# RWKV feed-forward: two explicitly mixed rows from GpSimd in place of doubled products, and a moved receptance product

## The chip, the cores and the metric

The kernel runs on one core of one Trainium2 chip, as one launch. The metric is the device time of that launch in microseconds (us). Differences of less than about 0.3% can't be told from no change. In the text TensorE is PE, VectorE is DVE, ScalarE is ACT, GpSimd is POOL; "L1948" is line 1948 of the kernel before.

## The reference, cut to what matters

The program is a chain of four networks (cross attention with an MLP, an instance-norm attention, a second cross attention with an MLP, an RWKV block) over x of 16 sequences x 64 tokens x 256 channels. The change lies in the last one, the RWKV block, and there in its feed-forward half:

```python
def step(s, rkvw):
    r_t, k_t, v_t, w_t = rkvw
    a = k_t[..., :, None] * v_t[..., None, :]
    out = jnp.einsum('bhi,bhij->bhj', r_t, u * a + s)
    s = a + w_t[..., :, None] * s
    return (s, out)
...
og = ((og - m) / jnp.sqrt(va + 1e-05)).reshape(b, l, e) * gn_w + gn_b
x1 = x + og * g @ Wo.T
xc = _ln(x1, ln2_w, ln2_b)
sx2 = jnp.concatenate([state[:, 0:1] - xc[:, :1], xc[:, :-1] - xc[:, 1:]], axis=1)
xk2 = xc + sx2 * ffn_maa_k
xr2 = xc + sx2 * ffn_maa_r
rr = jax.nn.sigmoid(xr2 @ Wfr.T)
kk = jnp.square(jax.nn.relu(xk2 @ Wfk.T))
return x1 + rr * (kk @ Wfv.T)
```

`sx2` is the row before minus the row itself; `xk2` and `xr2` are the two mixed rows.

## The kernel before, in words

Everything but the inputs and outputs stays in SBUF. The 1024 rows are cut into 8 tiles of 128 rows (two sequences of 64), numbered 0 to 7 (`LAST` = 7). The five engines run their own programs, written out by hand in one order each, and are tied by semaphores: a step increments its signal (`did(i)`), and whoever needs it waits (`at(i)`). Each engine works strictly in its written order, so a wait holds all that stands behind it.

The RWKV part is a software pipeline over slots. In one slot PE works at several tiles at once; in the loop of `rwkv_tensor` (from L2130) it runs gather(slot-3), turn(slot), decay2 and spread1(slot-2), center(slot-3), ffn_keys and ffn_receive(slot-5), project(slot-1), turn_heads(slot-3), ffn2(slot-5), lora(slot), turn_ffn(slot-4), attended(slot-3), decay1(slot-1), mixes(slot), spread0(slot-1). The last tiles leave the loop and are finished by a straight list (L2160 to L2187), in which ffn_keys(5) stands ahead of gather(7), and whose `warm` calls (L270) are products whose result nobody reads.

The names the text needs:
- DVE, `rwkv_vector`: products0/products1 (L2457), bonus (L2498), out_heads (L2503), mix2 (L2441), group_sum (L2510), scan0/scan1 (L2476, 3 and 5 scans), group_rstd and group_norm (L2516, L2523), receive (L2492, the receptance times the scans of its 5 heads), gate (L2450), attended (L2529, makes x1), ffn and close (L2537, L2543), mix1 (L2433).
- ACT, `rwkv_scalar`: heads (L2265, gives `y`), f_stats (L2307 to L2311), f_normed (L230), square and std (L2253, L2258), ffn_rows (L2275, writes `xc`), relu, receive and relu_square (L2282, L2289, L2294).
- POOL, `rwkv_gpsimd`: f_rstd (L2616 to L2620), first (L2650), receive (L2657, the receptance times the scans of the other 3 heads, `rs0`), f_state (L2643), gated (L2664, which lets PE's attended start), bonus (L2671, `ruk`).

The feed-forward before the change needs no mixed row. Since xc + (xs - xc) f = xc (1-f) + xs f with xs the row before, POOL scales the weights once, early in the program (`rwkv_consts_gpsimd`, L1935 to L1940), and PE multiplies the same buffer `xc` (64 rows and the one before them, for two sequences) twice, read at offset 1 with W(1-f) and at offset 0 with Wf:

```python
ffn_parts = [(m.wr[:, W_FK, :, :], m.wr[:, W_FR, :, :], k, 1) for k in range(KD)]\
    + [(m.wfks, m.wfrs, k, 0) for k in range(KD)]
```

So ffn_keys is 8 products of 128x128 and ffn_receive is 8 products of 64 stationary columns by 256. In a trace each f32 product leaves two records.

turn_ffn(i) writes a PSUM bank that the tile before uses, and waits until DVE's ffn(i-1) has read it (`rf`, L2087).

## Time and profile before

| what | value |
|---|---|
| time, median of 3 runs (all) | 982.9 us (982.54, 982.9, 985.4) |
| span of the profiled execution | 982.8 us |
| PE busy / PE weight load busy | 944.6 (96%) / 795.7 (81%) |
| DVE / ACT / POOL busy | 592.1 (60%) / 462.5 (47%) / 411.8 (42%) |
| chain that ended last | PE 74%, DVE 12%, ACT 5%, issue 4%, POOL 4% |
| RWKV part | from about 807 us to the end |

Of the profiled execution the page gives the span alone; its 982.8 us is 0.1 us from the median run. The page cuts the span into busy shares, follows back the chain of work that ended last, and lists groups of instructions with what ended the idle time before them. Matmuls are pipelined and their ends are modelled, so the weight load is read beside PE's busy time.

### The profile page before, as it was taken

The page shows a single profiled execution, that of the slowest core. Times are in us where ns is not written, and L with a number is a line of the kernel's source. Part 1 is how long each engine was busy: PE and PEld are TensorE (multiplying, and loading weights), DVE is VectorE, ACT ScalarE, POOL GpSimd, SP SyncE. Part 2 cuts the span into 40 slices and gives each one's busy share as a digit, 9 for nine tenths or more (in the row PEclk, how much of TensorE's full clock was granted, in tenths as well). Part 3 has the DMA queues.
Part 4 walks back from the last instruction along what each step waited for, and adds up shares of the span by engine and source line. Part 5 has one row for each costly group of instructions (what it writes and reads, how often), then busy time and mean ns, then how long its engine had stood idle before and what let it go on. Part 6 is the DMA issues. An engine that isn't in the chain of part 4 may idle for free.

```text
span 982.8 us, 21494 instructions
## 1 busy us (share of the span) xinstructions
PE 944.6 (96%) x8321; PEld 795.7 (81%) x8321; DVE 592.1 (60%) x974; ACT 462.5 (47%) x1026; POOL 411.8 (42%) x572
## 2 busy tenths in 40 slices
PE   6999999989999999999999999999999999999998
PEld 4777777966788888988897888998888888678776
DVE  5899986767544433344356433344426766999883
ACT  4677874237643333333334333333342434576565
POOL 2143346875365333333246343342422862344231
PEclk9999999999999999999999999999999999999999
DMA  9100000310011110111101110111100100000000
GB/s 298 37 23 2 2 2 22 116 54 2 1 55 50 54 50 25 37 54 48 54 7 55 50 54 21 42 49 48 54 22 18 41 14 1 1 2 6 13 6 23
DMA packets 24147, 37.15 MB, mean 38 GB/s; under 512 B 4432, under 2 KB 16528, under 8 KB 23824
## 3 DMA queue, kind: packets, MB, share of 16 engines
q1 hardware_dynamic: 24080, 36.23, 11.9%
q8 instruction: 45, 0.74, 0.3%
q14 instruction: 22, 0.18, 0.1%
HBM read 35.17 MB, written 1.05 MB: 37 GB/s over the span
## 4 chain that ended last, share of the span: by engine, by line
PE 74%; DVE 12%; ACT 5%; issue 4%; POOL 4%; DMA 0%; DVEq 0%; ACTq 0%; POOLq 0%
PE ps L1292 18%; PE ps L790 13%; PE ps L1309 9%; PE ps L1351 6%; PE ps L1948 5%; PE ps L890 4%; PE ps L1327 4%; PE ps L1337 2%; DVE sb L2476 2%; DVE sb L656 1%; PE ps L270 1%; DVE sb L650 1%; PE ps L2026 1%; PE ps L421 1%; PE ps L2112 1%
## 5 line engine op out<-in xcount | busy, mean ns | idle before, releaser
L837 POOL TENSOR_TENSOR sb<-sb 128x256 fp32r<-128x256 f32 (+1 forms) x128 | 102.5, 801 | 278.0 <-DMA sb<-in_heads_a 144.9
L1292 PE MATMUL ps<-sb 128*128 128x512 f32 x768 | 187.7, 396 | 1.0 <-issue 1.0
L1292 PEld LDWEIGHTS ps<-sb 128*128 128x128 f32 x768 | 139.5, 188 | 33.0 <-ACT sb L1425 3.1
L790 PE MATMUL ps<-sb 128*128 128x256 f32 x1152 | 148.4, 286 | 0.0
L790 PEld LDWEIGHTS ps<-sb 128*128 128x128 f32 x1152 | 141.4, 191 | 2.1 <-issue 0.2
L839 POOL TENSOR_TENSOR sb<-sb 128x256 fp32r<-128x256 f32 (+1 forms) x128 | 115.8, 905 | 10.0
L1522 DVE SCALAR_TENSOR_TENSOR sb<-ps,sb 128x512 fp32r<-128x512 f32 x64 | 45.1, 747 | 95.6 <-ACT sb L1458 95.5
L1309 PE MATMUL ps<-sb 128*128 128x256 f32 x768 | 99.2, 285 | 0.4 <-DVE sb L1490 0.4
L1502 DVE TENSOR_REDUCE sb<-ps 128x8 f32<-128x520 f32 x32 | 22.4, 700 | 126.6 <-PE ps L1327 126.6
L1309 PEld LDWEIGHTS ps<-sb 128*128 128x128 f32 x768 | 95.0, 191 | 3.0 <-issue 0.9
L1425 ACT ACTIVATE sb<-ps,sb 128x512 f32<-128x512 f32 x64 | 43.8, 685 | 107.9 <-PE ps L1292 107.8
L1948 PE MATMUL ps<-sb 128*128 128x128 f32 (+2 forms) x576 | 79.5, 290 | 3.9 <-DVE sb L2457 1.8
L1948 PEld LDWEIGHTS ps<-sb 128*128 128x128 f32 (+1 forms) x576 | 69.7, 185 | 12.9 <-issue 6.7
L1458 ACT ACTIVATE sb<-ps,sb 128x512 fp32r<-128x512 f32 x64 | 40.5, 684 | 80.6 <-PE ps L1351 80.6
L1490 DVE TENSOR_TENSOR sb<-ps,sb 128x512 f32<-128x512 f32 x64 | 43.9, 690 | 37.6 <-PE ps L1309 37.3
L1351 PEld LDWEIGHTS ps<-sb 64*128 64x128 f32 x1024 | 59.7, 188 | 8.1 <-issue 5.1
L1351 PE MATMUL ps<-sb 64*128 64x64 f32 x1024 | 64.1, 275 | 0.0
L2476 DVE TENSOR_TENSOR_SCAN sb<-sb 128x256 f32<-128x256 f32 x64 | 51.3, 863 | 0.0
L1442 ACT ACTIVATE sb<-ps,sb 128x512 f32<-128x512 f32 x64 | 43.4, 679 | 14.9 <-PE ps L1292 14.8
L1447 ACT ACTIVATE sb<-sb 128x520 f32<-128x520 f32 x32 | 20.5, 640 | 63.1 <-DVE sb L1504 63.1
L890 PE MATMUL ps<-sb 128*128 128x512 f32 x192 | 47.9, 403 | 0.0
L222 POOL TENSOR_TENSOR sb<-sb 128x1 f32<-128x1 f32 x24 | 13.3, 554 | 81.7 <-DVE sb L606 74.0
(221 smaller groups left out, 1668.2 us busy)
## 6 DMA issues: line engine op xcount, KB each, us to landing
sb<-in_heads_a SPq DMA_DIRECT2D x32, 386.0 KB, 3.0
sb<-in_heads_c SPq DMA_DIRECT2D x16, 256.0 KB, 3.6
...
```

The source lines that it names most:

```text
L790: last = pe.matmul(m.acc(t), lhsT[x], rhs[w], start=opens and n == 0, stop=False, skip_group_check=True)
L837: pool.tensor_tensor(high, src, one, ALU.mult).then_inc(*G.did(name + "_high", u))
L839: pool.tensor_tensor(low, src, high.bitcast(F32), ALU.subtract).then_inc(*G.did(name, u))
L890: last = pe.matmul(m.ps[u][:, at, :], m.w_parts[u][w][:, (r % 2 * KD + k) * P:(r % 2 * KD + k + 1) * P], m.h_parts[x][:, k, c * 512:(c + 1 ...
L1292: last = pe.matmul(m.ps[u][:, c, :], m.w_parts[u][w][:, (KD * q + k) * P:(KD * q + k + 1) * P], rows[x][:, k, c * 512:(c + 1) * 512], star ...
L1309: last = pe.matmul(m.ps[u0][:, c0, b * 2 * P:(b + 1) * 2 * P], m.enc_parts[x][:, k, (2 * j + b) * P:(2 * j + b + 1) * P], m.wv_parts[w][:, ...
L1351: last = pe.matmul(m.ps[1 - u][:, o, j * P + b * S:j * P + (b + 1) * S], m.v[j // 2][half, 2 * (j % 2) + b, u, :], m.pT[u][half, j, b * S: ...
L1425: act.activation(head_keys_of(m, u)[:, 8 * c:8 * c + 8, 0:S], m.ps[u][:, c, :].rearrange("p (n k) -> p n k", k=S), ACT.Identity, bias=m.he ...
L1490: vec.tensor_tensor(dst, m.ps[u0][:, c0, :].rearrange("p (b c) -> p b c", b=2), bc(m.v_row[:, :], 1, [P, 2, 2 * P]), ALU.add).then_inc(*hd ...
L1522: vec.scalar_tensor_tensor(out=m.ctx_low(u, o), in0=m.ctx_ps(u, o), scalar=m.bv[u][:, :], in1=m.ctx_high(u, o).bitcast(F32), op0=ALU.add, ...
L1948: last = pe.matmul(out, lhsT, rhs, start=n == 0, stop=n == len(terms) - 1)
L2476: last = vec.tensor_tensor_scan(m.sc[:, j, :], m.wS[i % 2][:, :, :].rearrange("p n s -> p (n s)"), m.av[:, j, :, :].rearrange("p n s -> p ...
```

## The change

`xc` gets a companion: for each tile two full mixed rows are written into a new buffer `xkr` (two of them, by tile parity, in the place of the scaled weights), with `sx2` as scratch. For tiles 0 to 5 POOL makes them (one subtraction of 128x256, one product and one sum of 128x512), at the end of its slot; for tiles 6 and 7 (`BY_VECTOR`) DVE does (one subtraction of 128x256 and four fused multiply-adds of 128x128), at two places of its closing list. PE then has 4 products of 128x128 for the keys and 2 of 128 stationary columns by 256 for the receptance, both behind the new signal `xkr`. POOL's receptance product (`receive`) moves behind `gated` in each slot. The early scaling of the weights goes, but for `headsum_u`. `ffn_rows` and `f_state` of the next tile wait for `xkr` of the last instead of for its receptance product.

```diff
+BY_VECTOR = range(LAST - 1, TILES)
@@ rwkv_consts_gpsimd
-    pool.tensor_tensor(m.wfks, m.wr[:, W_FK, :, :], wide("ffn_k", D), ALU.mult)
-    pool.tensor_tensor(m.wfrs, m.wr[:, W_FR, :, :], wide("ffn_r", D), ALU.mult)
     pool.tensor_tensor(m.headsum_u, bc(m.headsum[:, :], 1, [P, KD, P]), wide("u", P), ALU.mult).then_inc(m.s_scaled, 1)
-    pool.wait_ge(m.s_scaled, 1)
-    pool.tensor_tensor(m.wr[:, W_FK, :, :], m.wr[:, W_FK, :, :], m.wfks, ALU.subtract)
-    pool.tensor_tensor(m.wr[:, W_FR, :, :], m.wr[:, W_FR, :, :], m.wfrs, ALU.subtract).then_inc(m.s_scaled, 1)
@@ rwkv_tensor
     def ffn_keys(i):
-        pe.wait_ge(*done["xc"].at(i))
-        pe.wait_ge(*done["f_state"].at(i))
+        pe.wait_ge(*done["xkr"].at(i))
         for e in range(KD):
             last = product(m.key_bank(i)[:, e * P:(e + 1) * P],
-                           [(wk[:, k, e * P:(e + 1) * P], m.xc[:, k, :, s:s + S]) for wk, _, k, s in ffn_parts])
+                           [(m.wr[:, W_FK, k, e * P:(e + 1) * P], m.xkr[i % 2][:, 0, k, :]) for k in range(KD)])
...
-        for n, (_, wr, k, s) in enumerate(ffn_parts):
-            for b in range(2):
-                last = pe.matmul(m.receive_bank(i)[b * S:(b + 1) * S, D:2 * D], m.xc[:, k, b, s:s + S], wr[:, k, :],
-                                 start=n == 0, stop=n == len(ffn_parts) - 1)
-        last.then_inc(*done["kk_rr"].did(i))
+        product(m.receive_bank(i)[:, D:2 * D],
+                [(m.xkr[i % 2][:, 1, k, :], m.wr[:, W_FR, k, :]) for k in range(KD)]).then_inc(*done["kk_rr"].did(i))
@@ rwkv_scalar, ffn_rows
-            act.wait_ge(*done["kk_rr"].at(i - 1))
+            act.wait_ge(*done["xkr"].at(i - 1))
@@ rwkv_vector
+    def ffn_mix(i):
+        vec.wait_ge(*done["xc"].at(i))
+        vec.wait_ge(*done["f_state"].at(i))
+        if i == BY_VECTOR[0]:
+            vec.wait_ge(*done["xkr"].at(i - 1))
+        vec.tensor_tensor(m.sx2..., rows[:, :, 0:S], rows[:, :, 1:S + 1], ALU.subtract)
+        vec.wait_ge(*done["kk_rr"].at(i - 2))
+        for f, name in enumerate(("ffn_k", "ffn_r")):
+            for k in range(KD):
+                last = vec.scalar_tensor_tensor(out=split(m.xkr[i % 2][:, f, k, :]), in0=split(m.sx2[:, k, :]),
+                                                scalar=m.col(name, k), in1=m.xc[:, k, :, 1:S + 1], op0=ALU.mult,
+                                                op1=ALU.add)
+        last.then_inc(*done["xkr"].did(i))
@@ the closing list
     group_norm(LAST)
+    ffn_mix(LAST - 1)
     attended(LAST)
-    for i in (LAST - 2, LAST - 1, LAST):
+    ffn(LAST - 2)
+    close(LAST - 2)
+    ffn_mix(LAST)
+    for i in (LAST - 1, LAST):
         ffn(i)
         close(i)
@@ rwkv_gpsimd
     def f_state(i):
-            pool.wait_ge(*done["kk_rr"].at(i - 1))
+            pool.wait_ge(*done["xkr"].at(i - 1))
+    def ffn_mix(i):
+        pool.wait_ge(*done["xc"].at(i))
+        pool.wait_ge(*done["f_state"].at(i))
+        pool.tensor_tensor(m.sx2..., rows[:, :, 0:S], rows[:, :, 1:S + 1], ALU.subtract)
+        if i >= 2:
+            pool.wait_ge(*done["kk_rr"].at(i - 2))
+        pool.tensor_tensor(m.xkr[i % 2], bc(m.sx2, 1, [P, 2, KD, P]), bc(factors, 3, [P, 2, KD, P]), ALU.mult)
+        pool.tensor_tensor(mixed, mixed, bc(rows[:, :, 1:S + 1], 1, [P, 2, 4, S]), ALU.add)\
+            .then_inc(*done["xkr"].did(i))
@@ the loop over slots
         first(slot - 4)
+        gated(slot - 5)
         receive(slot - 4)
         f_state(slot - 6)
-        gated(slot - 5)
         bonus(slot - 3)
+        ffn_mix_early(slot - 6)
```

On POOL, one slot of the closing part (the one with gated(6) and the first 3 heads' product of tile 7). Before; `rwkv_y` is ACT's heads, `rwkv_scan0` DVE's first three scans:

```order
L2616 TENSOR_SCALAR sb<-sb 128x1 [waits attn0_rows_eps]
L2618 TENSOR_TENSOR sb<-sb 128x1 [waits gpsimd_own]
L2620 TENSOR_TENSOR sb<-sb 128x1 [waits gpsimd_own]
L2650 COPY sb<-sb 128x32 [waits rwkv_scan1]
L2657 TENSOR_TENSOR sb<-sb 128x768 [waits rwkv_scan0]
L2643 COPY sb<-sb 128x4 [waits rwkv_kk_rr]
L2664 TENSOR_TENSOR sb<-sb 128x256 [waits rwkv_gate,rwkv_y]
```

The same slot with the change (`attn0_ctx` is the semaphore that carries `xkr`):

```order
L2629 TENSOR_SCALAR sb<-sb 128x1 [waits attn0_rows_eps]
L2631 TENSOR_TENSOR sb<-sb 128x1 [waits gpsimd_own]
L2633 TENSOR_TENSOR sb<-sb 128x1 [waits gpsimd_own]
L2687 COPY sb<-sb 128x32 [waits rwkv_scan1]
L2701 TENSOR_TENSOR sb<-sb 128x256 [waits rwkv_gate,rwkv_y]
L2694 TENSOR_TENSOR sb<-sb 128x768 [waits rwkv_scan0]
L2657 COPY sb<-sb 128x4 [waits attn0_ctx]
L2664 TENSOR_TENSOR sb<-sb 128x256 [waits rwkv_f_state,rwkv_xc]
L2670 TENSOR_TENSOR sb<-sb 128x512 [waits rwkv_kk_rr,gpsimd_own]
L2674 TENSOR_TENSOR sb<-sb 128x512 [waits gpsimd_own]
```

The product for 3 heads now follows gated, and the three instructions of the mix end the slot.

On PE, the closing list around gather(7), before: attended(6), ffn_keys(5), gather(7).

```order
L1948 MATMUL ps<-sb 128x256 [waits rwkv_gated]
L1948 MATMUL ps<-sb 128x256
L1948 MATMUL ps<-sb 128x128 [waits rwkv_f_state,rwkv_xc]
L1948 MATMUL ps<-sb 128x128 x7
L2050 MATMUL ps<-sb 128x128 [waits rwkv_x1,rwkv_ruk]
L2050 MATMUL ps<-sb 128x128
L2056 MATMUL ps<-sb 32x256 [waits rwkv_rs1,rwkv_rs0]
```

With the change:

```order
L1944 MATMUL ps<-sb 128x256 [waits rwkv_gated]
L1944 MATMUL ps<-sb 128x256
L1944 MATMUL ps<-sb 128x128 [waits attn0_ctx]
L1944 MATMUL ps<-sb 128x128 x3
L2046 MATMUL ps<-sb 128x128 [waits rwkv_x1,rwkv_ruk]
L2046 MATMUL ps<-sb 128x128
L2052 MATMUL ps<-sb 32x256 [waits rwkv_rs1,rwkv_rs0]
```

The order is the same; ffn_keys(5) has half the products and another wait.

## Rows read from the trace of the kernel before

**Rows 1.** The page, chain that ended last: share of the span by engine.
```profile
PE 74%; DVE 12%; ACT 5%; issue 4%; POOL 4%; DMA 0%; DVEq 0%; ACTq 0%; POOLq 0%
```

**Rows 2.** Windows: stretch, its length, PE, weight load, DVE, ACT, POOL busy (count); clock, DMA.
```profile
888.00:906.70 18.70, 18.70 (x160) 14.94 (x159) 16.84 (x26) 12.87 (x34) 6.89 (x13) 1.00 0.02 8
```

**Rows 3.** Chain that ended last, slot 6 (start us, us, what): keys, then receptance.
```profile
897.93 1.79 PE ps L1948 x16
899.72 1.88 PE ps L2112 x16
```

**Rows 4.** Timeline, slot 6: start us, us, engine, line [idle before <-releaser].
```profile
902.38 4.16 DVE L2476 TENSOR_TENSOR_SCAN sb<-sb 128x256 f32<-128x256 f32 x5
906.49 0.42 DVE L2537 SCALAR_TENSOR_TENSOR sb<-sb,ps 128x256 f32<-128x256 f32 x1
906.82 1.77 DVE L2492 TENSOR_TENSOR sb<-sb 128x1280 f32<-128x1280 f32 x1
907.48 1.70 POOL L2671 TENSOR_TENSOR sb<-sb 128x256 f32<-128x256 f32 x1 [0.23 <-ACT sb L2234]
907.85 0.44 PE L2089 MATMUL ps<-sb 128*128 128x128 f32 x2
909.19 0.42 DVE L2529 TENSOR_TENSOR sb<-ps,sb 128x256 f32<-128x256 f32 x1 [0.27 <-PE ps L1948]
911.30 1.49 DVE L2433 TENSOR_TENSOR sb<-ps,sb 128x1280 f32<-128x1280 f32 x1 [1.36 <-PE ps L1987]
```

**Rows 5.** Timeline, slot 4, the same POOL line; then all scans: duration ns min/median/max.
```profile
870.31 0.72 POOL L2671 TENSOR_TENSOR sb<-sb 128x256 f32<-128x256 f32 x1 [0.97 <-ACT sb L2234]
...
L2476 DVE TENSOR_TENSOR_SCAN sb<-sb x64: 657/665/2235, 831.7 to 958.6; 128x256 f32<-128x256 f32 x64
```

**Rows 6.** By source line, POOL's 128x512 product and difference: ns min/median/max, first and last start.
```profile
L1936 POOL TENSOR_TENSOR sb<-sb x1: 1490/1490/1490, 312.4 to 312.4; 128x512 f32<-128x512 f32 x1
...
L1939 POOL TENSOR_TENSOR sb<-sb x1: 1282/1282/1282, 314.6 to 314.6; 128x512 f32<-128x512 f32 x1
```

**Rows 7.** Timeline, closing part, tiles 4 to 7.
```profile
946.34 0.79 ACT L2275 ACTIVATE sb<-ps,sb 128x128 f32<-128x128 f32 x2
...
948.49 0.19 POOL L2616 TENSOR_SCALAR sb<-sb 128x1 f32<-128x1 f32 x1 [2.18 <-ACT sb L2311]
...
950.62 0.59 ACT L230 ACTIVATE sb<-sb 128x256 f32<-128x256 f32 x1
...
951.35 0.38 ACT L2253 ACTIVATE sb<-ps 128x256 f32<-128x256 f32 x1
...
951.84 0.41 DVE L2510 TENSOR_REDUCE sb<-sb 128x32 f32<-128x256 f32 x1
...
954.10 1.82 POOL L2657 TENSOR_TENSOR sb<-sb 128x768 f32<-128x768 f32 x1 [4.34 <-DVE sb L2476]
...
955.60 0.80 ACT L2265 ACTIVATE sb<-ps,sb 128x128 f32<-128x128 f32 x2
...
959.52 1.47 DVE L2492 TENSOR_TENSOR sb<-sb 128x1280 f32<-128x1280 f32 x1
...
961.14 1.07 PE L2056 MATMUL ps<-sb 128*32 128x256 f32 x16 [0.15 <-DVE sb L2492]
...
962.27 0.42 DVE L2498 TENSOR_TENSOR sb<-ps,sb 128x256 f32<-128x256 f32 x1 [0.49 <-PE ps L2056]
```

**Rows 8.** Timeline: DVE's two fused multiply-adds of 128x128; ACT's last ffn_rows; PE's last ffn2.
```profile
899.38 0.62 DVE L2421 SCALAR_TENSOR_TENSOR sb<-sb 128x128 f32<-128x128 f32 x2
...
973.78 0.81 ACT L2275 ACTIVATE sb<-ps,sb 128x128 f32<-128x128 f32 x2
...
978.67 1.13 PE L1948 MATMUL ps<-sb 128*128 128x256 f32 x4
```

**Rows 9.** Windows, PE alone: stretch, length, busy (count), granted clock, DMA share, GB/s.
```profile
762.90:764.60 1.70, 0.00 (x0) 1.00 0.00 0
766.00:769.70 3.70, 3.70 (x11) 0.54 0.00 0
```

More of the change, by code:

```diff
@@ L2090, in turn_ffn @@
         last.then_inc(*done["f_turned"].did(i))
-    ffn_parts = [(m.wr[:, W_FK, :, :], m.wr[:, W_FR, :, :], k, 1) for k in range(KD)]\
-        + [(m.wfks, m.wfrs, k, 0) for k in range(KD)]
     @of_tile
     def ffn_keys(i):
-        pe.wait_ge(*done["xc"].at(i))
-        pe.wait_ge(*done["f_state"].at(i))
+        pe.wait_ge(*done["xkr"].at(i))
         for e in range(KD):
             last = product(m.key_bank(i)[:, e * P:(e + 1) * P],
-                           [(wk[:, k, e * P:(e + 1) * P], m.xc[:, k, :, s:s + S]) for wk, _, k, s in ffn_parts])
+                           [(m.wr[:, W_FK, k, e * P:(e + 1) * P], m.xkr[i % 2][:, 0, k, :]) for k in range(KD)])
         last.then_inc(*done["kk_raw"].did(i))
@@ L2529, in attended @@
         vec.tensor_tensor(m.x[:, i, :], m.c0[:, 0:D], m.x[:, i, :], ALU.add).then_inc(*done["x1"].did(i))
+    def ffn_mix(i):
+        rows = m.xc[:, :, :, :].rearrange("p k b s -> p (k b) s")
+        split = lambda x: x.rearrange("p (b s) -> p b s", b=2)
+        vec.wait_ge(*done["xc"].at(i))
+        vec.wait_ge(*done["f_state"].at(i))
+        if i == BY_VECTOR[0]:
+            vec.wait_ge(*done["xkr"].at(i - 1))
+        vec.tensor_tensor(m.sx2.rearrange("p k (b s) -> p (k b) s", b=2), rows[:, :, 0:S], rows[:, :, 1:S + 1],
+                          ALU.subtract).then_inc(*m.own_vec.did("sx2", i))
+        vec.wait_ge(*m.own_vec.at("sx2", i))
+        vec.wait_ge(*done["kk_rr"].at(i - 2))
[5 more added lines that the diff above has]
+        last.then_inc(*done["xkr"].did(i))
     @of_tile
@@ L2641, in f_state, with ffn_mix_early @@
         if i >= 1:
-            pool.wait_ge(*done["kk_rr"].at(i - 1))
+            pool.wait_ge(*done["xkr"].at(i - 1))
         pool.tensor_copy(m.xc[:, :, :, 0], state(i, 0)).then_inc(*done["f_state"].did(i))
+    def ffn_mix(i):
+        rows = m.xc[:, :, :, :].rearrange("p k b s -> p (k b) s")
+        pool.wait_ge(*done["xc"].at(i))
+        pool.wait_ge(*done["f_state"].at(i))
+        pool.tensor_tensor(m.sx2.rearrange("p k (b s) -> p (k b) s", b=2), rows[:, :, 0:S], rows[:, :, 1:S + 1],
+                           ALU.subtract).then_inc(*m.own_pool.did("sx2", i))
+        pool.wait_ge(*m.own_pool.at("sx2", i))
+        if i >= 2:
+            pool.wait_ge(*done["kk_rr"].at(i - 2))
+        factors = m.colbuf[:, COL["ffn_k"]:COL["ffn_k"] + 2 * KD].rearrange("p (f k) -> p f k", f=2)
+        pool.tensor_tensor(m.xkr[i % 2], bc(m.sx2, 1, [P, 2, KD, P]), bc(factors, 3, [P, 2, KD, P]), ALU.mult)\
+            .then_inc(*m.own_pool.did("sxf", i))
+        pool.wait_ge(*m.own_pool.at("sxf", i))
+        mixed = m.xkr[i % 2].rearrange("p f k (b s) -> p f (k b) s", b=2)
+        pool.tensor_tensor(mixed, mixed, bc(rows[:, :, 1:S + 1], 1, [P, 2, 4, S]), ALU.add)\
+            .then_inc(*done["xkr"].did(i))
+    @of_tile
+    def ffn_mix_early(i):
+        if i not in BY_VECTOR:
+            ffn_mix(i)
     @of_tile
@@ L2807, in build @@
         scaled = lambda at, n: consts[:, at:at + KD * n].rearrange("p (k n) -> p k n", k=KD)
-        m.wfks, m.wfrs, m.headsum_u = (
-            scaled(at, n) for at, n in ((0, D), (KD * D, D), (KD * 2 * D, P)))
+        m.xkr = [consts[:, at:at + 2 * D].rearrange("p (f k n) -> p f k n", f=2, k=KD) for at in (0, KD * D)]
+        m.headsum_u = scaled(KD * 2 * D, P)
+        m.sx2 = scaled(KD * (2 * D + 3 * P), P)
         m.xl = [scaled(at, P) for at in (KD * (2 * D + P), KD * (2 * D + 2 * P))]
@@ L2876, in build @@
         m.tile_done["kk_raw"] = Signal(m.done["ctx_ps"].sem, len(ITEMS))
+        m.tile_done["xkr"] = Signal(m.done["ctx"].sem, len(ITEMS))
         m.own_vec, m.own_act, m.own_pool = (Own(sem(n)) for n in ("vector_own", "scalar_own", "gpsimd_own"))
@@ L3012, in _ @@
             mlp_tensor(pe, ph["mlp2"], m, 12, HALVES[:-LATE])
-            rwkv_tensor(pe, m, ph["mlp2"], 12, [(m.s_scaled, 2)])
+            rwkv_tensor(pe, m, ph["mlp2"], 12, [(m.s_scaled, 1)])
 def lay_out(inputs):
```

## The prediction

> **What bounds the kernel now.** I read the page first: the chain that ended last is PE's to 74%, DVE's to 12% [rows 1]. The change touches nothing before 807 us but five lines of POOL at 311 us, so I then cut the RWKV part into slots. In a middle slot of 18.7 us PE is busy all of it and DVE 16.84 us [rows 2]. In the chain the middle slots are PE alone, one row after another; the keys and the receptance stand in it with 1.79 and 1.88 us per tile [rows 3]. The timeline of the slot shows how close the others are: DVE waits only twice, 0.27 us for attended and 1.36 us for mixes [rows 4]. So the middle is PE's with DVE 1.6 us behind.
>
> The Trainium skill (Perfetto Trace Analysis, Identifying the Most-Contended Engine) holds PE's weight load, not its busy time, for the measure of how full it is. By that the slot is 14.94 of 18.7 us, 80% [rows 2], less full than it looks; the sum below goes by DVE's waits and needs neither.
>
> The closing part is a chain over all engines: DVE's scans and product (959.52), gather(7) on PE (961.14), bonus on DVE (962.27) [rows 7], then gate by gate to the last ffn2 at 978.67 [rows 8].
>
> **The change part by part.**
>
> *The products.* Keys go from 8 products to 4, receptance from 8 of half width to 2 of full width, that is half of 1.79+1.88 [rows 3]: about 1.85 us less of PE per tile.
>
> *What a middle slot gains.* Not 1.85: DVE's two waits are 1.63 us in all, and a second bound stands in front. turn_ffn(i) waits for DVE's ffn (L2537, at 906.49), which stands behind the five scans; it now runs at 907.85 [rows 4]. A slot can thus shrink by 907.85 - 906.49 - 0.42 = 0.94 us before PE waits there. POOL adds to that. Its product L2671 takes 0.72 us alone and 1.70 us beside DVE's two-input L2492, which itself takes 1.77 us against 1.47 elsewhere [rows 4, 5, 7]; one scan takes 0.665 us in the median and up to 2.235 [rows 5]. So instructions of POOL and of DVE with two SBUF inputs hold each other up. The moved receptance product (1.82 us, [rows 7]) now meets L2492 instead of the scans: DVE's scans gain perhaps 0.5 us and L2492 loses up to 1.8. And f_rstd now stands behind the mix, about 1 us late, so f_normed, and behind it on ACT square, and then group_sum on DVE, slip by some 0.3 to 0.6. I take 0.65 us per slot for the two full slots and 0.6 for the slot after them (there DVE waits 0.57 for PE): **-1.9 us**; ends -4 (all of DVE's waits go, with the scans' gain) and +0.5 (POOL's blocking eats it).
>
> The Trainium skill (SBUF, SBUF: two separate sides) says of the port pair that the two engines share that the loser "fully blocks" for a whole instruction. The pair 0.72 and 1.70 us agrees; by that rule, with one meeting of the 1.8 us product and L2492 per slot, the slots would gain nothing and the sum would be 1.9 us higher.
>
> *The mix on POOL.* No row shows it. The nearest are its own 128x256 product (0.72, [rows 5]) and the 128x512 product and difference of the constants (1.49 and 1.28, [rows 6]): 3.5 us a tile with the two own waits between; ends 3.2 and, where L2492 stands in the way, 5. In middle slots it starts when `xc` is there and ends some 2 us ahead of ffn_keys; hidden, with f_rstd queued behind it as counted.
>
> *Tile 4's mix, closing part.* `xc`(4) is there at 947.13, the mix ends at 950.7. f_rstd(5), begun at 948.49, now begins there: 1.1 us later it lets f_normed(5) start at 951.8 instead of 950.62; square(6) comes at 952.4 instead of 951.35 and group_sum(6) at 952.9 instead of 951.84 [rows 7]. DVE's scans for tile 7 stand behind it: the chain is **1.1 us** late, and ACT's heads(6) starts at 956.7 instead of 955.60.
>
> *Tile 5's mix.* This is the large one. POOL's order is now gated(6), receive(7), f_state(5), mix(5). gated(6) waits for heads(6) (957.5) and for a scan under way, and ends near 958.9; receive(7) takes 1.82 plus one scan's blocking, to 961.2; L2492, due at 960.6, holds POOL to 962.6; the mix ends at 966.2. On PE ffn_keys(5) stands ahead of gather(7): 0.95 us, then gather with 1.7 us, so that DVE's bonus starts at 968.9 instead of 962.27 [rows 7]: **+6.6 us**, the 1.1 above in it. Lower end: no late group_sum and no blocking, 956.4 + 0.75 + 1.82 + 0.2 + 3.3 + 2.65 = 965.1, +2.9. Upper end: L2492 of tile 6 is held by POOL's product too, another 1.4, +8.
>
> *PE's clock.* With keys(5) late PE stands idle some 6 us behind attended(6). The trace has such a case: PE is idle for 1.7 us up to 764.6, and from 766.0 on, though busy without a gap, it has a mean of 0.54 of its clock for 3.7 us, the lower of the levels 1.2 and 2.4 GHz [rows 9]. That costs 3.7 x 0.46 = 1.7; It would fall on keys(5), gather(7) and center(7), all on the chain: **+1.7**, ends 0 and +3.8 (a second gap).
>
> *Tiles 6 and 7 on DVE.* One subtraction (0.42) and four multiply-adds (0.62 for two, [rows 8]) are about 1.8 us. For tile 6 they stand ahead of attended(7), waiting for `xc`(6), which ACT makes after heads(7): x1(7) slips by **0.3**. For tile 7 `xc` is there at 974.59 [rows 8]; then mix 1.85, keys and receptance 1.9 in place of 0.3 of waiting and 3.77 of products: **-0.25**.
>
> *The constants.* POOL loses 4 instructions of about 1.3 us at 311 us [rows 6]; the next ones wait for DMA and for PE there, so nothing. If that cover were gone it would be a gain of at most 5 us of POOL time, none of it on the chain.
>
> Sum: -1.9 + 6.6 + 1.7 + 0.3 - 0.25 = +6.45. On the profiled execution's 982.8 that is 989.25; the median of the runs is 0.1 above it: **989.3 us**.
>
> **The rivals.**
> - *The middle pays for the end* (no measurable change, within 0.3%, which is about what can be told from no change): slots gain 4, the end loses its lower 2.9 and no clock, up to the case gain 2, loss 4.5. 982 to 985.8 us. For it: DVE's 1.36 us waits are plain in the rows, and my blocking is counted from few meetings. Against: ffn_keys(5) ahead of gather(7) is in the order itself, and the moved product is in front of the mix. 0.22.
> - *PE's time counts in full* (faster): the middle is PE's to the last tenth [rows 2]; if turn_ffn's bound moves with the scans, four slots give 1.6 us each, and the end gives back its 1.85 us for tiles 4 and 7 while POOL gets tile 5's rows done by 962. It decides for this case if xkr(5) is ready before about 961.5, when gather(7) is due: then 982.9 - 6.5 - 1 + 0.5 = 976 us, or 979 with half of it. Against: gated(6) can't start before heads(6) at 956.4, and 1.82 + 3.3 us come behind it. 0.08.
> - *POOL slows the middle too*: blocking of L2492 and late group_sum exceed 1.6 us per slot. Then 989.3 + 1.9 + 1 = 992.2 us. For it: the 2.235 us scan [rows 5]. 0.15.
> - *The clock holds*, 987.6 us: it lies in the forecast's case.
>
> **How the numbers follow.** Forecast 0.55 (986 to 991.5), rivals as above. Faster 0.08, same 0.22, slower 0.70. The range that leaves out 2 in 10 reaches from 984.0 into the balance case to 993.0.
>
> **What would show it.** In the changed profile: slots of 18.0 us where 18.75 stand; PE no longer full in them, with a wait for DVE's ffn ahead of turn_ffn; POOL's mix of 3.5 us ending 2 us ahead of ffn_keys; group_sum(6) about 1 us late; PE idle some 6 us for POOL's L2674 ahead of ffn_keys(5), the longest wait of the part, with the clock at 0.5 behind it; from bonus(7) to the end 18 to 20 us as before. It is wrong if ffn_keys(5) does not wait for POOL, or if the slots stay at 18.75, or shrink to 17.

## The result

The changed kernel takes 989.96 us, median of 5 runs (989.55 to 991.39), against 982.9 (982.54 to 985.4) before: ratio 1.0059, 95% interval 1.0040 to 1.0077. The forecast was 989.3, slower. So the number is right, and the sections below show that this is in part luck: two of its terms were off by 2.4 to 3.2 us in opposite directions. The profiled execution is the longest of the five (span 989.6; the other four 987.7 to 988.3); a likely reason is in its trace and is told at the end of this section.

The page of the changed kernel, in answer to [rows 1]: span, busy time, and the chain that ended last.

```profile
span 989.6 us, 21204 instructions
PE 936.9 (95%) x8161; PEld 790.2 (80%) x8161; DVE 592.1 (60%) x984; ACT 462.1 (47%) x1026; POOL 430.2 (43%) x586
PE 63%; POOL 12%; DVE 11%; issue 8%; ACT 6%; DMA 0%; POOLq 0%; DVEq 0%; ACTq 0%
```

80 products fewer (160 records), and POOL's share of the chain goes from 4% to 12%, PE's from 74% to 63%. To see where, I follow one marker, DVE's bonus of each tile (L2498 before, L2488 after), through the RWKV part. Its starts for tiles 0 to 7 are, before: 842.62, 859.35, 876.53, 895.28, 914.04, 932.79, 949.04, 962.27; after: 843.36, 860.13, 878.72, 895.94, 913.15, 930.37, 944.67, 966.54. The last instruction of DVE starts at 980.29 and 987.03. Three stretches follow:

| stretch | before | after | difference | forecast |
|---|---|---|---|---|
| start of the part (bonus of tile 0) | 842.62 | 843.36 | +0.74 | 0 |
| bonus(0) to bonus(6), the middle | 106.42 | 101.31 | -5.11 | -1.9 |
| bonus(6) to bonus(7), the closing part | 13.23 | 21.87 | +8.64 | +6.6 and +1.7 |
| bonus(7) to the last close | 18.02 | 20.49 | +2.47 | +0.3 - 0.25 |

*The middle.* A full slot (from the bonus of tile 2 to that of tile 5 there are three) goes from 18.75 to 17.2 us, not to 18.0; the one behind them, bonus(5) to bonus(6), from 16.25 to 14.30. Windows over one slot, in answer to [rows 2]:

```profile
893.20:910.40 17.20, 16.67 (x140) 13.71 (x140) 16.97 (x26) 12.89 (x34) 11.25 (x16) 1.00 0.03 9
```

PE is busy for 16.67 of 17.2 us, DVE for 16.97: the slot is now DVE's (before, 18.70 and 16.84 of 18.7). Timeline of it, in answer to [rows 4] (the lines' numbers are ten lower: L2466 the scans, L2546 ffn, L2482 the receive rows, L2519 attended, L2423 mixes; on PE L2085 turn_ffn; on POOL L2694 the receive product and L2674 the mix's last; `...` marks rows left out):

```profile
903.02 3.51 DVE L2466 TENSOR_TENSOR_SCAN sb<-sb 128x256 f32<-128x256 f32 x5
...
906.46 0.39 DVE L2546 SCALAR_TENSOR_TENSOR sb<-sb,ps 128x256 f32<-128x256 f32 x1
906.77 2.72 DVE L2482 TENSOR_TENSOR sb<-sb 128x1280 f32<-128x1280 f32 x1
...
909.74 0.41 DVE L2519 TENSOR_TENSOR sb<-ps,sb 128x256 f32<-128x256 f32 x1
...
910.43 1.48 DVE L2423 TENSOR_TENSOR sb<-ps,sb 128x1280 f32<-128x1280 f32 x1
...
905.94 2.20 POOL L2694 TENSOR_TENSOR sb<-sb 128x768 f32<-128x768 f32 x1
...
912.18 1.19 POOL L2674 TENSOR_TENSOR sb<-sb 128x512 f32<-128x512 f32 x1
...
906.99 0.41 PE L2085 MATMUL ps<-sb 128*128 128x128 f32 x2 [0.53 <-DVE sb L2546]
```

Both waits of DVE are gone (0.27 and 1.36), the five scans take 3.51 instead of 4.16, L2482 takes 2.72 instead of 1.77 beside the moved product, and PE waits 0.53 for ffn ahead of turn_ffn, as forecast.

*The closing part.* Timeline, in answer to [rows 7]:

```profile
948.21 0.60 ACT L230 ACTIVATE sb<-sb 128x256 f32<-128x256 f32 x1 [1.86 <-POOL sb L2633]
...
949.11 0.42 DVE L2500 TENSOR_REDUCE sb<-sb 128x32 f32<-128x256 f32 x1 [1.55 <-ACT sb L2242]
...
953.72 1.15 POOL L2701 TENSOR_TENSOR sb<-sb 128x256 f32<-128x256 f32 x1 [5.37 <-ACT sb L2254]
954.82 2.19 POOL L2694 TENSOR_TENSOR sb<-sb 128x768 f32<-128x768 f32 x1
956.97 1.52 POOL L2657 COPY sb<-sb 128x4 f32<-128x4 f32 x1
958.63 0.61 POOL L2664 TENSOR_TENSOR sb<-sb 128x256 f32<-128x256 f32 x1
959.32 1.10 POOL L2670 TENSOR_TENSOR sb<-sb 128x512 f32<-128x512 f32 x1
960.50 1.17 POOL L2674 TENSOR_TENSOR sb<-sb 128x512 f32<-128x512 f32 x1
...
961.73 2.07 PE L1944 MATMUL ps<-sb 128*128 128x128 f32 x8 [5.15 <-POOL sb L2674]
...
964.59 1.87 PE L2052 MATMUL ps<-sb 128*32 128x256 f32 x16
...
966.54 0.43 DVE L2488 TENSOR_TENSOR sb<-ps,sb 128x256 f32<-128x256 f32 x1 [7.02 <-PE ps L2052]
```

group_sum(6) waits 1.55 us for ACT, which waits for POOL's f_rstd (L2633) behind the mix of tile 4. Then PE waits 5.15 us for the mix of tile 5, gather(7) follows behind its keys at 963.60, and DVE stands 7.02 us. The mix itself (958.63 to 961.67) takes 3.0 us. Windows, PE alone (stretch, length, busy, granted clock, DMA share, GB/s):

```profile
954.00:958.00 4.00, 2.58 (x7) 0.75 0.00 0
960.00:966.00 6.00, 4.27 (x28) 0.50 0.06 22
980.00:986.00 6.00, 4.95 (x16) 0.50 0.06 22
```

The clock is at its lower level, 1.2 of 2.4 GHz, not once but three times (953 to 956, 960 to 966, 980 to 986); the last time it hits the keys, receptance and products of tile 7, behind which nothing is left to hide it. The forecast had one fall of 1.7 us, and a second only as an upper end.

*The profiled execution.* The slot from the bonus of tile 1 to that of tile 2 takes 18.59 us in this trace. Six other traces, below, of kernels with the same order there (in y2 with a mix of one column) have 17.38 or 17.39 (before: 17.18); in this one the clock is 0.50 at 864 to 866. I take the 1.2 us for an event of this execution, since the other four are 1.3 to 1.9 us shorter; that is argued, for they left no trace. The middle's gain without it is 6.3 us.

### The profile page after: what moved, and what is told of

It reads as the page before. It is cut to its first block, busy times and chain, and to the rows that moved or that the text cites. A ratio compares the mean times of both kernels' runs of the same rounds, so it can differ in the third digit from the quotient of the medians.

```text
span 989.6 us, 21204 instructions
## 1 busy us (share of the span) xinstructions
PE 936.9 (95%) x8161; PEld 790.2 (80%) x8161; DVE 592.1 (60%) x984; ACT 462.1 (47%) x1026; POOL 430.2 (43%) x586
## 3 DMA queue, kind: packets, MB, share of 16 engines
HBM read 35.17 MB, written 1.05 MB: 37 GB/s over the span
## 4 chain that ended last, share of the span: by engine, by line
PE 63%; POOL 12%; DVE 11%; issue 8%; ACT 6%; DMA 0%; POOLq 0%; DVEq 0%; ACTq 0%
PE ps L1292 18%; PE ps L790 12%; PE ps L1309 9%; PE ps L1351 6%; PE ps L1327 4%; PE ps L890 2%; PE ps L1944 2%; PE ps L1337 2%; POOL sb L837 1%; POOL sb L2694 1%; DVE sb L656 1%; POOL sb L839 1%; PE ps L270 1%; DVE sb L650 1%; PE ps L421 1%
## 5 line engine op out<-in xcount | busy, mean ns | idle before, releaser
L1292 PE MATMUL ps<-sb 128*128 128x512 f32 x768 | 187.8, 396 | 1.0 <-issue 1.0
L1944 PE MATMUL ps<-sb 128*128 128x128 f32 (+2 forms) x544 | 85.1, 312 | 10.1 <-POOL sb L2674 5.2
L1944 PEld LDWEIGHTS ps<-sb 128*128 128x128 f32 (+1 forms) x544 | 72.6, 196 | 19.5 <-POOL sb L2674 5.9
L890 PE MATMUL ps<-sb 128*128 128x512 f32 x192 | 46.7, 394 | 0.7 <-DVE sb L1024 0.6
L270 PE MATMUL ps<-sb 128*128 128x512 f32 x129 | 42.4, 456 | 3.3 <-POOL sb L2987 3.3
```

The lines of the kernel that those rows point to most:

```text
L270: pe.matmul(bank, x[:, 0:P], x, start=True, stop=True)
L890: last = pe.matmul(m.ps[u][:, at, :], m.w_parts[u][w][:, (r % 2 * KD + k) * P:(r % 2 * KD + k + 1) * P], m.h_parts[x][:, k, c * 512:(c + 1 ...
L1292: last = pe.matmul(m.ps[u][:, c, :], m.w_parts[u][w][:, (KD * q + k) * P:(KD * q + k + 1) * P], rows[x][:, k, c * 512:(c + 1) * 512], star ...
L1944: last = pe.matmul(out, lhsT, rhs, start=n == 0, stop=n == len(terms) - 1)
```

## The experiments

All twelve were timed against the kernel before, run beside them on three chips, where it has a median of 985.0 to 985.4 us; so only ratios are compared between kernels, and stretches within traces. Each row's stretches are those of one execution. "Before" and "changed" stand there again for reading. A: bonus(0) to bonus(6); slot: a middle one; B: bonus(6) to bonus(7); C: bonus(7) to the last close; all us.

| kernel | A (slot) | B | C | A+B+C | ratio to before (95%) |
|---|---|---|---|---|---|
| before | 106.42 (18.75) | 13.23 | 18.02 | 137.67 | 1 |
| changed | 101.31 (17.22) | 21.87 | 20.49 | 143.67 | 1.0059 (1.0040 to 1.0077) |
| x1_gather_first | 100.13 (17.22) | 14.97 | 24.09 | 139.19 | 1.0009 (0.9992 to 1.0026) |
| x2_mix5_vector | 100.13 (17.22) | 18.50 | 20.40 | 139.03 | 1.0010 (0.9993 to 1.0027) |
| x3_receive_first | 109.91 (20.4) | 16.80 | 19.35 | 146.06 | 1.0091 (1.0063 to 1.0118) |
| x4_fill_idle | 100.12 (17.21) | 19.77 | 18.21 | 138.10 | 0.9998 (0.9984 to 1.0012) |
| y1_before_gated_first | 107.81 (18.75) | 18.61 | 18.01 | 144.43 | 1.0080 (1.0056 to 1.0103) |
| y2_small_mix | 100.11 (17.21) | 17.98 | 20.49 | 138.58 | 1.0014 (1.0002 to 1.0027) |
| y3_rstd_first | 100.09 (17.21) | 20.92 | 19.31 | 140.32 | 1.0045 (1.0025 to 1.0064) |
| z1_old_order_small_mix | 111.30 (20.4) | 13.21 | 19.70 | 144.21 | 1.0091 (1.0061 to 1.0121) |
| z2_state_first | 106.52 (18.75) | 13.32 | 18.03 | 137.87 | 0.9999 (0.9982 to 1.0015) |
| x5_no_constants | 106.42 (18.75) | 13.22 | 18.02 | 137.66 | 1.0004 (0.9988 to 1.0019) |
| c1_new_order | 100.10 (17.21) | 14.69 | 18.85 | 133.64 | 0.9972 (0.9956 to 0.9989) |
| c2_new_order | 100.54 (17.40) | 13.73 | 18.85 | 133.12 | 0.9973 (0.9958 to 0.9987) |

In x3 and z1 only the second and third of the three full slots are 20.4 us; the first is 18.84 and 18.83. The expected times below are by the kernel before at 982.9 us. The ratios times 982.9 give x1 983.8, x2 983.9, x4 982.7 and y3 987.3 us, each under its expected range (985 to 987, 986 to 987.5, 986 to 988, 988 to 988.7), and y1 990.8, over its own (982 to 984). c2's ratio misses 0.9960 to 0.9968. For z1 no time was expected. The other five are inside.

### Is it the place in PE's queue? (x1_gather_first)

```diff
 PE:   attended(LAST - 1)
-      ffn_keys(LAST - 2)
       gather(LAST); warm(m.td_ps, 3); center(LAST)
+      ffn_keys(LAST - 2)
 ACT:  f_stats(LAST - 1)
-      relu(LAST - 2); relu_square(LAST - 2)
-      table(ACT.Sqrt); f_normed(LAST - 1); square(LAST)
+      table(ACT.Sqrt); square(LAST)
       std(LAST); table(ACT.Tanh)
+      relu(LAST - 2); relu_square(LAST - 2); f_normed(LAST - 1)
```

> The changed kernel, with the keys of tile 5 behind gather(7) and center(7) on PE, and relu(5), its square and f_normed(6) behind square(7) and std(7) on ACT; POOL's mix of tile 5 stays where it is. Theory (the place in PE's queue makes the 7.02 us wait in front of the last bonus): gather(7) starts when DVE and POOL have made its rows, near 958.5 to 959 instead of 963.6, the last bonus stands at 961.5 to 962.5 instead of 966.54, and the time is 985 to 987 us; the keys come beside work that PE would else idle through. Rival 1 (DVE's chain is late by itself, because group_sum(6) waits for POOL's f_rstd behind the mix): the last bonus stands no earlier than 965.5, time 989 or more. Rival 2 (the whole loss of the closing part is this one place, clock included): 983 us or less.

B falls from 21.87 to 14.97, 1.74 above before: nearly the whole loss of the closing part hangs on keys(5) standing ahead of gather(7) while they wait for POOL. But C grows by 3.6. Timeline of PE and DVE in x1:

```profile
956.00 0.42 DVE L2488 TENSOR_TENSOR sb<-ps,sb 128x256 f32<-128x256 f32 x1 [0.18 <-PE ps L2052]
...
961.66 0.45 PE L2085 MATMUL ps<-sb 128*128 128x128 f32 x2 [2.46 <-ACT sb L230]
```

turn_ffn(6) now waits 2.46 us for f_normed(6) behind relu(5), and turn_heads(7), whose rows are there at 959.7, stands behind it until 963.6; the clock is at 0.50 behind that wait, from 962 to 965, and again under the last keys and products. So the ratio falls by 0.5% and not by the 6.9 us of B. The theory holds for the place; its sizes do not: the last bonus comes 14.97 us behind that of tile 6 where 16.8 to 17.8 were expected, and by its time x1 is nearer to rival 2 (983 or less).

### Is it POOL? (x2_mix5_vector)

```diff
-BY_VECTOR = range(LAST - 1, TILES)
+BY_VECTOR = range(LAST - 2, TILES)
     scan1(LAST)
+    ffn_mix(LAST - 2)
     attended(LAST - 1)
```

> The changed kernel, with the mixed rows of tile 5 made by DVE (one subtraction, four multiply-adds, about 1.8 us, between scan1(7) and attended(6)); POOL's last mix is tile 4's. Theory: PE's 5.15 us wait for POOL's L2674 goes; DVE's own chain (attended(6), then the product of receive(7)) is 1.8 us later, so that gather(7) starts near 960.5 and the last bonus at 963 to 963.8 instead of 966.54: 986 to 987.5 us. Rival 1 (DVE's chain is what is late): nothing or a loss, 990 or more. Rival 2 (POOL's gated and receive are held up by its mix of tile 4 and by DVE's new two-input instructions): 989 with L2657 and L2694 late.

B is 18.50, 3.37 less, within what was expected, and the ratio 1.0010. What remains over before, 5.27 us, is in part DVE's: its first mix instruction starts at 955.36, 1.83 us behind the scans, since f_state(5), which it reads, is ready only at 955.28 behind POOL's receive product. PE then waits 2.36 us for DVE's mix, and its clock is at 0.50 for the 3 us behind that. This pointed at the next question.

### Is the idle clock on the chain? (x4_fill_idle)

```diff
     attended(LAST - 1)
+    warm(m.td_ps, 16)
     ffn_keys(LAST - 2)
...
     ffn_receive(LAST - 1)
+    warm(m.td_ps, 5)
     turn_ffn(LAST)
     ffn2(LAST - 1)
+    warm(m.td_ps, 4)
     ffn_keys(LAST)
```

> The changed kernel with products of PE that nothing reads put into its three long waits of the end: 16 ahead of the keys of tile 5, 5 ahead of turn_ffn(7), 4 ahead of the keys of tile 7. Theory (PE's idle time in front makes the granted clock fall to 0.5 at 954 to 966 and at 980 to 986, and this is on the chain at both places): the clock stays above 0.9 in both stretches, the work from keys(5) to the last bonus is 1 to 2 us shorter and that from keys(7) to the end 2 to 2.5 shorter: 986 to 988 us. Rival 1 (the clock falls there for another reason, or was not on the chain): the time stays at 989.5 to 990.5. Rival 2 (the added products themselves delay the keys and ffn2): 990.5 us or more.

```profile
960.00:966.00 6.00, 4.86 (x36) 1.00 0.00 0
```

The same work, in the same order, with 25 products added that nothing reads: clock 1.00 where it was 0.50 (this row is x4's window of PE), B 2.10 less, C 2.28 less, ratio 0.9998. The clock alone is worth 4.4 of the 11.1 us that B and C lose in the changed kernel. The fall at 950 to 952 of x4's trace stays (0.50); into the wait of 2.75 us ahead of it nothing was filled.

### What does POOL's new order do by itself? (x3_receive_first, y1_before_gated_first)

x3 is the changed kernel with the old order; y1 the kernel before with the new one. The same three lines in both, in opposite directions:

```diff
 (y1)
+        gated(slot - 5)
         receive(slot - 4)
         f_state(slot - 6)
-        gated(slot - 5)
```

> The changed kernel with only POOL's order undone: receive and f_state ahead of gated again, the mix still last. Theory (the reordering matters little in the middle, where DVE sets the slot of 17.2 us; the product moved back to the scans slows them by 0.5 and frees L2482 of 1.2): slots of 16.8 to 17.4 us; in the closing part gated(6) is behind receive(7) and heads(6) to attended(6) 1 to 2 us later. Time 990 to 992 us. Rival 1 (the moved product in front of L2482 is what DVE's dense slot suffers from): slots of 16.5 and less, 986 us. Rival 2 (the slots' gain came from the reordering, not from PE's halved products): slots back at 18 us or more, 993 us or more.

> The kernel before with POOL's new order alone: gated ahead of receive and f_state, the doubled products and no mix. Theory (in the middle PE is the bound at 18.75 us a slot, and the order only moves POOL's long product off DVE's scans): DVE's five scans take about 3.5 us instead of 4.15, it waits the longer for PE, and the slots stay at 18.6 to 18.8 us; in the closing part the gated product is up to 1.8 us earlier, and receive(7) up to 1 later. 982 to 984 us by the kernel before at 982.9, ratio 0.999 to 1.001. Rival 1 (the order gives most of what the middle gained): slots of 17.9 us or less, 977 to 979 us. Rival 2 (L2492 held up by the long product makes DVE the bound at once): slots of 19 or more, 985 or more.

In x3 my theory fell: two of the three full slots are 20.4 us, 1.65 longer than *before* the change although PE has 1.85 us less to do, and the first is 18.84. The time (by the ratio 991.8 us) is in the expected range all the same, by luck. In y1 the middle went as expected (18.75, PE the bound), so rival 2 of x3, that the order alone gave the gain, is out too: the order gives nothing alone, and neither do the halved products. But y1's closing part, in which I expected no loss, costs 5.38 us without any mix. Timeline of y1 (L2664 gated, L2657 receive product, L2643 f_state; on PE the keys of tile 5), and its clock:

```profile
956.30 1.10 POOL L2664 TENSOR_TENSOR sb<-sb 128x256 f32<-128x256 f32 x1 [6.73 <-ACT sb L2265]
957.35 2.19 POOL L2657 TENSOR_TENSOR sb<-sb 128x768 f32<-128x768 f32 x1
959.49 1.45 POOL L2643 COPY sb<-sb 128x4 f32<-128x4 f32 x1
...
961.09 3.75 PE L1948 MATMUL ps<-sb 128*128 128x128 f32 x16 [2.50 <-POOL sb L2643]
```
```profile
960.00:966.00 6.00, 4.92 (x24) 0.52 0.08 25
```

A copy of 128x4 values behind a 2.19 us product holds the keys of tile 5 by 2.5 us; then the clock falls, and keys that take 1.95 us take 3.75.

### Does the state's place explain it? (z2_state_first)

```diff
-        receive(slot - 4)
         f_state(slot - 6)
         gated(slot - 5)
+        receive(slot - 4)
```

> The kernel before with POOL's order f_state, gated, receive (the new order gated, receive, f_state without the state's place behind the product). Theory (the 5.4 us that the new order alone costs in the closing part come from f_state(5) behind the receive product of tile 7, for which the keys of tile 5 wait, and from the clock that falls in that wait): from the bonus of tile 6 to that of tile 7 13.2 to 14 us instead of 18.61, the slots stay at 18.75, the clock does not fall behind 958: 982 to 984 us, ratio 0.999 to 1.002. Rival (the late receive product itself holds gather(7)): 16 us or more there, 986 or more.

B 13.32, slots 18.75, ratio 0.9999: the new order costs nothing once f_state stands ahead of it. The 5.3 us were one copy's place, the clock behind it included.

### What do the halved products do without order and mix? (z1_old_order_small_mix)

y2's kernel (below) with receive and f_state ahead of gated again.

> The changed kernel with POOL's old order (receive and f_state ahead of gated) and with the three mix instructions cut to one column each; it leaves out the mixing of tiles 0 to 5. What is left of the change is the halved products. Theory (the mix is hidden in a middle slot in either order, and the old order puts the long product on DVE's scans and gated's and bonus's behind it, so that DVE's ffn, for which PE's turn_ffn waits, comes late): slots of 19.5 to 20.4 us as with the whole mix in the old order (20.4), scans of 5 us. Rival 1 (the mix in the old order was what made the slots 20.4 us long): slots of 17.2 to 18.1 us, the 18.0 that the prediction reckoned among them. Rival 2 (the halved products give nothing without the order): 18.7.

18.83, 20.41 and 20.44 us for the three full slots, as in x3: the mix has no part in it. The first is not in the expected range (19.5 to 20.4) but beside the 18.7 of rival 2. Timeline of z1, one slot (POOL: product, f_state, gated, bonus; DVE: the five scans; PE: turn_ffn), and windows over the stretch behind it:

```profile
925.59 1.82 POOL L2694 TENSOR_TENSOR sb<-sb 128x768 f32<-128x768 f32 x1 [8.22 <-DVE sb L2466]
927.35 0.59 POOL L2657 COPY sb<-sb 128x4 f32<-128x4 f32 x1
928.15 0.91 POOL L2701 TENSOR_TENSOR sb<-sb 128x256 f32<-128x256 f32 x1 [0.21 <-ACT sb L2254]
929.12 1.00 POOL L2708 TENSOR_TENSOR sb<-sb 128x256 f32<-128x256 f32 x1
...
926.13 5.13 DVE L2466 TENSOR_TENSOR_SCAN sb<-sb 128x256 f32<-128x256 f32 x5
...
931.72 0.41 PE L2085 MATMUL ps<-sb 128*128 128x128 f32 x2 [2.15 <-DVE sb L2546]
```
```profile
931.00:933.00 2.00, 1.28 (x7) 0.93 (x8) 2.00 (x4) 0.00 (x0) 0.00 (x0) 0.99 0.02 4
933.00:935.00 2.00, 2.00 (x14) 1.67 (x16) 0.97 (x3) 0.94 (x4) 0.00 (x0) 0.50 0.07 25
```

Windows over the first and the second full slot of z1 (all engines), and PE's timeline in them:

```profile
879.79:898.62 18.83, 16.68 (x139) 13.72 (x139) 17.43 (x25) 12.82 (x33) 6.45 (x13) 1.00 0.02 8
898.62:919.03 20.41, 18.26 (x139) 15.13 (x140) 17.43 (x25) 11.61 (x28) 6.62 (x15) 0.92 0.02 8
```
```profile
892.46 0.41 PE L2085 MATMUL ps<-sb 128*128 128x128 f32 x2 [2.15 <-DVE sb L2546]
...
894.25 1.60 PE L1983 MATMUL ps<-sb 64*128 64x128 f32 x20
...
911.30 0.41 PE L2085 MATMUL ps<-sb 128*128 128x128 f32 x2 [2.15 <-DVE sb L2546]
...
913.55 2.71 PE L1983 MATMUL ps<-sb 64*128 64x128 f32 x20
```

With PE faster, ACT's heads come earlier, and so gated and POOL's bonus now fall on the scans behind the receive product: 5.13 us for five scans against 3.51 in the changed kernel, which has the product behind them. ffn is late, and PE waits 2.15 us. That wait is the same in the first slot and in the second, but in the first the clock stays at 1.00 behind it and the slot is 18.83 us, 0.08 over before; in the second it is at 0.50 for some 3 us (the 20 products of mixes, L1983, take 2.71 us in z1 and up to 2.36 in x3 where they take 1.60), and the slot is 1.58 us longer. So the late ffn eats the whole gain of the halved products, and nearly all of the 1.65 us on top is the clock. Why it held in the first slot of both traces is open. Behind the wait of 0.53 us, in the changed kernel, it held in every slot. The order is thus what makes the halved products a gain: 17.2 us against 18.8 with the clock held in both, and 20.4 where it fell.

### What does the mix cost? (y2_small_mix, y3_rstd_first)

```diff
 (y2: the three instructions of the mix on one column each)
-        pool.tensor_tensor(m.xkr[i % 2], bc(m.sx2, ...), bc(factors, ...), ALU.mult)
+        pool.tensor_tensor(m.xkr[i % 2][:, 0, 0, 0:1], m.sx2[:, 0, 0:1], factors[:, 0, 0:1], ALU.mult)
 (y3: in the slot of tile 4's mix; f_rstd(5) skipped in the next)
         bonus(slot - 3)
+        if slot == LAST + 3:
+            f_rstd(slot - 5)
         ffn_mix_early(slot - 6)
```

> The changed kernel with POOL's three mix instructions cut to one column each; all waits and the order stand. It leaves out the mixing of tiles 0 to 5. Theory (the mix is hidden in the middle and is what is late in the closing part): slots stay at 17.2 us; group_sum(6) comes 1.5 us earlier against the bonus of tile 6, the keys of tile 5 no later than 957.5, the last bonus 3.5 to 5 us earlier, and with the clock held 6: 983 to 986 us. Rival 1 (the mix holds DVE up in the middle too): slots under 16.8 us and 980 or less. Rival 2 (gated, the receive product and f_state ahead of it are what is late, not the mix): 988 or more.

> The changed kernel with f_rstd(5) on POOL ahead of the mix of tile 4, in that one slot. Theory (group_sum(6) on DVE stands 1.55 us because the three small instructions of f_rstd stand behind a mix of 3 us): group_sum(6) comes 1.3 to 1.6 us earlier against the bonus of tile 6 and the same goes through to the last bonus: 988 to 988.7 us. Rival 1 (what is late there is hidden behind the keys of tile 5): no change, 989.5 to 990.5. Rival 2 (the clock, which falls in PE's wait at 946 to 948, then stays up as well): 986 to 987.5.

y2: the slots stay at 17.21, so the mix is hidden in the middle. B falls by 3.89, to 17.98; the keys of tile 5 still wait 3.47 us for POOL, where the small mix stands behind f_state (954.11 for 1.45) and that behind the receive product, and the clock is still at 0.57 from 956 to 962: 4.75 of the 8.64 us come without mixing, which is my own rival 2 of this run, in part. C does not move, 20.49. In both y2 and y3 group_sum(6) comes 2.80 us behind the bonus as before, and not 4.44: 1.64 us for f_rstd's place. Of it only 0.95 goes through to the last bonus in y3, for the next wait took 0.57 of it. Timeline of y3 (L2687 is POOL's copy first(7), now behind the mix of tile 4):

```profile
946.36 0.41 DVE L2500 TENSOR_REDUCE sb<-sb 128x32 f32<-128x256 f32 x1
...
947.34 1.86 DVE L2466 TENSOR_TENSOR_SCAN sb<-sb 128x256 f32<-128x256 f32 x3 [0.57 <-POOL sb L2687]
```

The scans of tile 7 start 3.78 us behind the bonus of tile 6 instead of 4.77, that is 0.99 earlier. C is 1.18 us shorter as well, since in it the clock is at 0.50 for about three microseconds and not six. Its ratio is 1.0045, 1.4 us under the changed kernel's, within the two intervals; the stretches say more than the ratio here.

### The constants (x5_no_constants)

```diff
-    pool.tensor_tensor(m.wfks, m.wr[:, W_FK, :, :], wide("ffn_k", D), ALU.mult)
-    pool.tensor_tensor(m.wfrs, m.wr[:, W_FR, :, :], wide("ffn_r", D), ALU.mult)
...
-    pool.tensor_tensor(m.wr[:, W_FK, :, :], m.wr[:, W_FK, :, :], m.wfks, ALU.subtract)
-    pool.tensor_tensor(m.wr[:, W_FR, :, :], m.wr[:, W_FR, :, :], m.wfrs, ALU.subtract).then_inc(m.s_scaled, 1)
```

> The kernel before without the four POOL instructions at 311 us that split the feed-forward's two weights (products and differences of 128x512 and like size); it leaves out the split of these weights. Theory (what follows them on POOL waits for other things): no change, 982.4 to 983.4 us by the kernel before at 982.9, ratio 0.999 to 1.001, and the RWKV part begins at the same time. Rival (they hold something at 311 us): up to 5 us less.

Ratio 1.0004 and every stretch as before. Nothing, as forecast.

### A version that keeps the gain (c1_new_order, c2_new_order)

```diff
 PE:   turn_ffn(LAST - 2)
+      warm(m.td_ps, 4)
       turn_heads(LAST - 1); ffn2(LAST - 3); warm(m.td_ps, 3); attended(LAST - 1)
-      ffn_keys(LAST - 2)
       gather(LAST); warm(m.td_ps, 3); center(LAST)
-      turn_ffn(LAST - 1); ffn_receive(LAST - 2); turn_heads(LAST); ffn2(LAST - 2); warm(m.td_ps, 3); attended(LAST)
+      ffn_keys(LAST - 2); turn_heads(LAST); ffn_receive(LAST - 2); turn_ffn(LAST - 1); attended(LAST); ffn2(LAST - 2); warm(m.td_ps, 3)
       ffn_keys(LAST - 1); ffn_receive(LAST - 1)
+      warm(m.td_ps, 3)
       turn_ffn(LAST); ffn2(LAST - 1)
+      warm(m.td_ps, 4)
 ACT:  as x1, with heads(LAST) ahead of relu(LAST - 2)
 DVE:  attended(LAST) ahead of ffn_mix(LAST - 1)
 POOL: as y3; c2 also: f_state ahead of gated, first(LAST) ahead of tile 4's mix
```

> A version put together from these: the changed kernel with f_rstd(5) ahead of the mix of tile 4, the keys of tile 5 behind gather(7), turn_heads(7) and attended(7) ahead of the feed-forward of tiles 5 and 6 on PE, ACT and DVE, and unread products in PE's waits (4 ahead of turn_heads(6), 3 ahead of turn_ffn(7), 4 ahead of the keys of tile 7). Theory (the middle's gain of 6 us stays if the closing part isn't held up by the mix, and the clock doesn't fall): last bonus 13 to 14.5 us behind that of tile 6, the end 18 to 20 us behind it: 977.5 to 981 us by the kernel before at 982.9, ratio 0.995 to 0.998. Rival (the feed-forward of three tiles, now all behind the last attention, makes PE and ACT the bound of the end): 22 us or more behind the last bonus, 983 or more.

> The version c1_new_order (ratio 0.9972) with two more moves on POOL: f_state ahead of gated in all slots, and the copy of first(7) ahead of the mix of tile 4, for which DVE's scan waited 0.56 us. Theory: the scans of tile 7 start 0.5 us earlier, the mix of tile 5 starts 0.6 earlier; the middle's slots stay at 17.2 us: 0.5 to 1 us less than c1_new_order, ratio 0.9960 to 0.9968. Rival (POOL's instructions only meet DVE's two-input instructions elsewhere): no change to c1_new_order or 0.5 us more.

c1 has B at 14.69 and C at 18.85, no clock fall behind 944, and A+B+C 4.0 us under before; its interval (0.9956 to 0.9989) excludes 1, though 0.28% is no more than the 0.3% that can hardly be told from no change. c1 and c2 are the only ones of these kernels whose interval lies below 1. c2's closing part is another 0.96 us shorter, but its slots are 0.2 longer: with f_state out of the way POOL's bonus meets DVE's L2485 and takes 1.97 us instead of 0.72. No difference in the ratio, as its rival said. c1's middle with c2's closing part was not tried.

## Why the prediction was right, and where it was not

- **What bounds the middle: right.** PE's products are the bound before (y1 leaves them and stays at 18.75), DVE is after.
- **The middle's size: wrong, -1.9 against -5.1 (-6.3 without the one event).** Two steps failed. One is the count of slots: I took two full ones and one behind them, and the traces have three and one. The other, and the larger, is the price of a slot, 0.65 us against 1.53 (0.6 against 1.95 in the last): I let DVE's L2492, held up by the moved product, eat most of the gain of the scans. It does take 2.72 instead of 1.77 us. But it stands behind ffn, for which PE waits, and DVE's two waits of 1.63 us lay behind it to take it up. The bound that counts is the one I had written down, 907.85 - 906.49 - 0.42 = 0.94, plus the 0.65 that the scans gain, 1.59; measured are 1.53. Even the lower end of this term, -4, was too near. Slots of 17.2 us are also closer to 17, which I had named as a sign of being wrong, than to the 18.0 forecast. The rival "the middle pays for the end", with a gain of 4, came nearest.
- **The Trainium skill's rule on the port pair: right on the meeting; the time that I worked out from it was wrong.** [Rows 4, 5] and the pairs below show that one engine waits for a whole instruction of the other, as the Trainium skill (SBUF, SBUF: two separate sides) says. By it, as I had reckoned it, the slots would have gained nothing; they gained 1.53, since the engine that is held up had waits behind. The weight load as the measure of PE, by the Trainium skill (Perfetto Trace Analysis, Identifying the Most-Contended Engine), gives 13.71 of 17.20, 80% as before. Against DVE's busy share, 90% before and 99% after, it points to DVE both times, which fits the slot after and not the one before.
- **The mix in the middle: right**, hidden (y2), and cheaper than forecast: 3.0 to 3.2 us a tile, not 3.5, which is the lower end or under it. In the slot before the one shown POOL ends it at 896.14, 2.3 us ahead of PE's products at 898.42.
- **Tile 4's mix: right in kind**, 1.64 us at group_sum instead of 1.1; with that undone the last bonus comes 0.95 earlier (y3).
- **Tile 5's mix and the clock, +6.6 and +1.7: right in sum (8.3 against 8.64), wrong in name.** The queue gated, receive, f_state, mix was counted, from the bonus of tile 6 to the end of the mix 17.2 us against 17.0 measured, but put down to the mix. y1 shows 5.38 us without a mix, all of it f_state's place (z2: 0.09), the mix itself 3.9 (y2). Both act through one wait, so they don't add up, and the clock is 2.1 of it (x4).
- **The end, +0.05 against +2.47: wrong.** The step that failed is that I let PE's clock fall only once, at tile 5. With half the products PE stands idle 1.53 us ahead of turn_ffn(7), for f_normed, and 1.20 ahead of keys(7), for the rows that DVE makes, and the clock is at 0.50 on the last 5 us of products. I had this as "a second gap", an end of the range. x4, with those waits filled, has C at 18.21, 0.19 over before. The 0.05 would have fitted only there. (The term for tile 7 had a slip too: its own numbers add up to -0.32 and not -0.25.)
- **Constants: right** (x5).

So against the 6.74 us between the two traces the forecast of +6.45 took 3.2 us too little gain in the middle, 2.4 too little loss at the end, 0.3 too little in the closing part, and nothing for the 0.7 by which the part starts later by chance. That these nearly cancel is luck. The mechanism of the loss, PE standing for POOL's L2674 ahead of gather(7), was forecast and shown; the number is better than its parts.

Open: why the clock held behind some waits of PE and not behind others of the same length, and why POOL's product in the changed kernel takes 2.20 us ahead of L2482, 0.38 more than the 1.82 beside scans.
